# Four stages of a small vision network on one core: further matmuls without a reader in TensorE's pauses between the triangle product and the recurrence

## The reference

```python
# third block, on x normalized
a = sigmoid((x @ Wa1 + ba1) * (x @ Wa2 + ba2)); b = sigmoid((x @ Wb1 + bb1) * (x @ Wb2 + bb2))
g = sigmoid(x @ Wg + bg)
z = einsum('bikc,bkjc->bijc', a, b)
x = x + g * (_ln(z, ln2_g, ln2_b) @ Wz + bz)      # _ln over the 16 channels of z
# fourth block, on x normalized
def step(carry, xw_t):                            # 28 steps
    h, c = carry
    zi, zf, zo, zg = split(xw_t + h @ Wm)
    c_new = sigmoid(zf) * c + sigmoid(zi) * tanh(zg)
    h_new = sigmoid(zo) * tanh(c_new)
```

## Time and profile before

| what | value |
|---|---|
| median of three runs | 473.28 us (470.24 to 478.76) |
| the profiled execution | 475.85 us |
| its span, first to last instruction | 474.1 us |
| mean granted clock over the span | 0.901 |
| TensorE matmuls busy | 351.1 us (74%) |
| VectorE busy | 365.1 us (77%) |
| ScalarE busy | 299.8 us (63%) |
| GpSimd (POOL) busy | 233.9 us (49%) |

### The profile page before, as it was taken

One profiled execution on the slowest core, in us unless ns is written; L12 is line 12 of the kernel. 1 busy time (PEld: TensorE's weight loads), 2 busy tenths in 40 slices (PEclk: granted clock), 3 DMA queues, 4 the chain that ended last, 5 costly groups with the idle time before them and its releaser, 6 DMA issues. The chain is left out here.

```text
span 474.1 us, 10021 instructions
## 1 busy us (share of the span) xinstructions
PE 351.1 (74%) x3480; PEld 230.4 (49%) x3480; DVE 365.1 (77%) x679; ACT 299.8 (63%) x583; POOL 233.9 (49%) x217
## 2 busy tenths in 40 slices
PE   5149888896789785985877647666795829888885
PEld 4037676675665332142233213222483519877774
DVE  3799999999797388799787999997576685544443
ACT  4327788887785899578758946347985253333432
POOL 4526868775673324966972999567081130000000
PEclk9997999998899999599897885768999668999999
DMA  6110000000223231022000000000030000111111
GB/s 147 5 18 3 3 1 0 0 1 0 59 60 70 51 87 29 1 60 58 1 0 1 0 1 0 0 0 1 3 68 3 1 0 11 20 19 22 22 19 24
DMA packets 24044, 10.29 MB, mean 22 GB/s; under 512 B 20576, under 2 KB 22368, under 8 KB 24016
## 3 DMA queue, kind: packets, MB, share of 16 engines
q1 hardware_dynamic: 23888, 9.93, 10.3%
q0 software_dynamic: 128, 0.01, 0.2%
HBM read 2.00 MB, written 1.61 MB: 8 GB/s over the span
## 5 line engine op out<-in xcount | busy, mean ns | idle before, releaser
L480 POOL TENSOR_TENSOR Pr<-Pr,rc 128x392 f32<-128x392 f32 x64 | 54.4, 883 | 32.2 <-DVE rc L1826 32.2
L511 POOL TENSOR_TENSOR YA<-YA,hC 128x784 f32<-128x784 f32 x27 | 51.7, 1914 | 32.4 <-DVE hC L1910 31.5
L1349 PE MATMUL pair<-BCf,sel 96*128 96x392 bf16 x128 | 38.4, 394 | 35.0 <-DVE Hs L1894 30.8
L1894 DVE TENSOR_TENSOR_SCAN Hs<-dA,pair 128x784 f32<-128x784 f32 x32 | 57.1, 1785 | 1.0
L1193 PE MATMUL pair<-ident,Pr 128*128 128x128 f32 x256 | 41.1, 293 | 13.2 <-ACT PT L715 9.0
L1349 PEld LDWEIGHTS pair<-BCf,sel 96*128 96x128 bf16 x128 | 10.2, 105 | 74.0 <-issue 71.6
L1193 PEld LDWEIGHTS pair<-ident,Pr 128*128 128x128 f32 x256 | 29.2, 146 | 25.1 <-ACT PT L715 15.8
L1887 DVE TENSOR_TENSOR pair<-DU,pair 128x784 f32<-128x784 f32 x32 | 31.1, 973 | 10.6 <-PE pair L1349 10.3
L715 ACT ACTIVATE PT<-pair 128x392 f32<-128x392 f32 x64 | 31.4, 497 | 5.9 <-PE pair L1193 5.6
L724 ACT ACTIVATE Pr<-Ts 128x392 f32<-128x392 f32 x64 | 32.5, 536 | 3.4 <-DVE Ts L1810 3.4
L1804 DVE TENSOR_REDUCE mx<-pair 128x8 f32<-128x392 f32 x64 | 32.6, 550 | 1.6 <-PE pair L1150 1.4
(11 more groups left out here) (262 smaller groups left out, 928.8 us busy)
## 6 DMA issues: line engine op xcount, KB each, us to landing
SX<-XP SPq DMA_DIRECT2D x48, 112.2 KB
XT<-in_x SPq DMA_DIRECT2D x4, 392.0 KB, 5.0
out<-Os SPq DMA_DIRECT2D x28, 56.0 KB, 1.8
AD<-Aa SPq DMA_DIRECT2D x4, 196.0 KB
NB<-in_L_conv_x_proj_w SPq DMA_DIRECT2D x4, 3.0 KB
DW<-in_L_conv_dw SPq DMA_DIRECT2D x4, 1.1 KB
vec<-in_L_conv_b_qkv POOLq DMA_DIRECT2D x3, 0.5 KB, 5.8
W<-in_L_conv_w_qkv SPq DMA_DIRECT2D x1, 48.0 KB
```

What stands on the lines that cost most here:

```text
L480: eng.tensor_tensor(pg, pg, bcast(rc[:, g, :], 2, WT), ALU.mult).then_inc(pn_r, 1)
L511: eng.tensor_tensor(y, y, hC[:, n % NHC, :], ALU.add).then_inc(g_ya, 1)
L1349: ins = eng.matmul(SPREAD[s][:, columns(h)], sel[:, n, :], upper(BCf[:, c % 2, s, columns(h)]), start=True, stop=True)
L1894: eng.tensor_tensor_scan(Hs[:, n % 2, :], dA[:, n % NA, :], SPREAD[0], 0.0, ALU.mult, ALU.add).then_inc(v_s, 1)
```

## The change

TensorE's program alone is changed. After `variance(1)` (t_v at 2) it issues nine matmuls of `spare` instead of three, then waits for t_c at 3 and issues five more. Between `turn_z(0)` and `turn_z(1)` it waits for t_v at 3 and issues eight. After `final(1)` it issues four groups of eight into bank 5: behind t_y at 4, behind `biases`, behind l_mv at 2, and behind l_mv at 3. Then, as before, it waits for the normalized data.

```diff
             eng.wait_ge(t_v, 1)
             spare(3, 7)
             eng.wait_ge(t_v, 2)
-            spare(3, 7)
+            spare(9, 7)
+            eng.wait_ge(t_c, 3)
+            spare(5, 7)
...
             eng.wait_ge(t_gd, 8)
             eng.wait_ge(t_n, 2)
             turn_z(0)
+            eng.wait_ge(t_v, 3)
+            spare(8, 7)
             eng.wait_ge(t_n, 3)
             eng.wait_ge(t_nd, 1)
             turn_z(1)
...
             eng.wait_ge(t_y, 4)
+            spare(8, 5)
             eng.wait_ge(t_ye, 4)
             biases(0, 0)
             biases(1, 1)
+            spare(8, 5)
+            eng.wait_ge(l_mv, 2)
+            spare(8, 5)
+            eng.wait_ge(l_mv, 3)
+            spare(8, 5)
             eng.wait_ge(l_xn, J - 1)
             eng.wait_ge(l_x3, 1)
             inputs(0, 0)
```

## The result

The changed kernel takes 472.98 us in the median of 22 executions (467.71 to 475.02). The kernel before, run as often, takes 476.94 us (470.24 to 479.19). The ratio is 0.9939, with a 95% interval of 0.9909 to 0.9968: about 2.9 us less, between 1.5 and 4.3. Taken from the two medians it is 4.0 us; the ratio says less because it leaves out the executions that were over 1.5% above the fastest of their kernel, nine before and four after. The three runs shown ahead of the prediction had a median of 473.28, so they were low by 3.7 us.

A forecast was written before the change was run, and what follows sets the result against it. The chain of waits lies mainly on VectorE here, passing through half-clock TensorE in two places. Gains of 2.5 us (`turn_z(1)`, `final`) and 1.1 us (recurrence) make 3.6; 473.28 - 3.6 = 469.7 us, range 465.3 to 475.0.

The forecast's parts named there:

- The clock is the mechanism, in two places: A faster TensorE helps at `turn_z(1)` with `final`'s first half, 2.5 us, and at the recurrence's first step, 1.1 us.
- `turn_z(1)` gained: The second transposes, before `final`, take at most 1.05 us instead of 1.73; 0.75 us gained with the pipeline's end.
- The first half of `final`: The first 64 records of `final`, 4.63 us at half clock, gain 1.75 us (1.5 to 2.0) at full clock.
- First inputs to gates: At the recurrence's start, 2.94 us becomes 1.86 as in step 2: 1.1 us gained, upper end 1.5.
- The costs put at zero: Added matmuls before `turn_z(0)`, between the transposes and behind `final` fit TensorE's pauses; bank conflicts and code loading also 0.
- The idle time in front of `turn_z(1)`: After the eight added matmuls, 0.7 us of slack remains before VectorE's scaling of the last image releases `turn_z(1)`.
- The sum for the median: Whole kernel: 2.5 + 1.1 = 3.6 us off the three runs' median of 473.28 gives 469.7 us.
- Rival 1: In the 1.8 to 1.9 us pause before the recurrence the clock falls again; 1.1 us lost, 470.8; chance 0.23.
- Rival 2: The clock falls before `final` all the same; only the recurrence's 1.1 us remain, 472.2; chance 0.10.
- Rival 3: Added matmuls at half clock delay the transposes in TensorE's order: +4.9 us, 478.2; chance 0.05.
- Rival 4: The transposes stay slow, `turn_z(1)` at 1.73 us; 2.85 us gained, 470.4; chance 0.02.
- Code loading: TensorE's longer program may add a stop like the 0.82 us one at its loop's entry: 0 to 0.8, taken as 0.

The follow-up runs named there:

- e1_front: The changed kernel without the four groups of eight behind `final`; ratio to the kernel before 0.9989 (0.9951 to 1.0026).
- e3_no_last: The changed kernel without its last group of eight, behind l_mv at 3; ratio to the kernel before 0.9990 (0.9949 to 1.0030).
- e2_back: The changed kernel with the front undone, only the four groups behind `final` added; ratio to the kernel before 1.0053 (1.0012 to 1.0093).
- e5_nine_more: The changed kernel with 18 instead of nine matmuls in the group after t_v at 2; one execution, 115.3 us from triangle product to end.
- e10_conv_only: The kernel before with 14 matmuls without a reader ahead of `conv(2)` and 12 within it; median 471.21 us, ratio to the kernel before 0.9929.
- e7_no_mid: The changed kernel without the eight matmuls between `turn_z(0)` and `turn_z(1)`; one execution, 117.3 us from triangle product to end.
- e11_conv_pause: The changed kernel with 14 matmuls in its last group and 14 in the pause ahead of `conv(2)`, none within it; ratio to the kernel before 0.9876.
- e8_last14: The changed kernel with 14 instead of eight matmuls in its last group; median of six 473.13 us, ratio to the kernel before 0.9857.

## Why the prediction was right or wrong

**The clock is the mechanism, in two places: right.** The two places add up in the trace: 2.55 us up to the first inputs, 1.3 us in the first step, 3.9 in all, where 2.5 + 1.1 = 3.6 was forecast. e1_front has the first without the second, and e3_no_last against the changed kernel shows the second by itself. e2_back was to show it too and did not, since the clock fell there all the same.

**The terms.** `turn_z(1)` gained 1.73 - 0.96 = 0.77 (forecast 0.75). The first half of `final` gained 4.63 - 2.83 = 1.80 (1.75), and VectorE kept up, as forecast: its four gatings run on in 2.54 us. Their row in the changed kernel:

```profile
376.24 2.54 DVE L2124 SCALAR_TENSOR_TENSOR Y<-pair,vec,Gt 128x392 f32<-128x392 f32 x4 [0.35 <-PE pair L1587]
```

First inputs to gates gained 2.94 - 1.63 = 1.31, not 1.1: in step 2, from which I took the 1.86 us, L1642 waits for the state (written until 397.86, L1642 starts at 397.92), which costs some 0.2 us that the first step does not need. The costs put at zero were zero: the transposes start 11.15 and 14.64 us behind the product, before 11.15 and 14.63. The idle time in front of `turn_z(1)` was 0.66 us (0.7 forecast), and e5_nine_more shows that the slack is real and finite.

**The sum for the median: the step that failed.** It reads "the forecast for a median is 473.28 - 3.6 = 469.7". The change of 3.6 us (ratio 0.9924) lies inside the measured interval, near the 4.0 between the medians and the 2.9 of the ratio. The level under it does not hold: 473.28 was the median of three executions, and 22 gave 476.94. The profiled execution, 475.85, was the nearer one, and 475.85 - 3.6 = 472.2 would have been 0.8 us off. Set against the level now known, 469.7 says 7.2 us less: 1.8 times the 4.0 us between the medians and 2.5 times the 2.9 us of the ratio. I used the spread of those runs to widen the range, which then held 472.98, and not to doubt the centre; that the range held is owed to its width. What spreads the runs was in the trace: the clock in the second block, at 5 tenths in slices 17 and 25, which the prediction passed over as "high through most of the span". In its place the runs showed a level that hangs on an earlier pause: with the pause in front of `conv(2)` filled and nothing else changed, the median is 471.21 against 474.71 of the kernel before beside it, and the scatter falls from 7.6 to 2.1 us (e10_conv_only). Not all of the scatter is explained by it; `conv(2)` itself begins anywhere from 186.4 to 189.0 us.

**Rival 1 (the clock falls again before the recurrence): it happens in some executions.** The rows named in its favour and against it, 1.81 us held and 2.18 us fell, were read as if a length of pause decided. It doesn't alone: a pause of 1.82 us in the same place held in the two profiles of the changed kernel and was followed by a fall in those of three kernels that differ from it ahead of the pause. I gave it 0.23 as an alternative for the median; it is rather a share of executions, and the three profiles lost 1.0 to 1.3 us each. That both profiles of the changed kernel held may be luck. What this takes from the gain of the whole time is not shown: the means of all 22 executions, 476.32 and 472.44, differ by 3.9 us, as much as the two tails, and with their scatter they could not tell 3.9 from 3.

**Rival 2** did not occur in any of ten profiles with both front groups, and occurred in full without the middle one (e7_no_mid). **Rival 3** did not occur; its mechanism, delay in order, is what e5_nine_more measured at full clock: 0.86 us for nine. **Rival 4**, by the rule of the Trainium skill (TensorE: Matmul & The Clock Gate, Part 4: PE-mode transpose), fell: seven took 0.96 us at a granted 1.00, so the trace does not agree with the page. Whether transposes alone would keep or raise the clock, no run here separates. **Code loading** cost nothing that shows: the stop at the loop's entry is 0.84 us, before 0.82.

## What to carry to other kernels

Cut the trace at the first changed instruction and compare from there; here the start of the product alone carries 6 us of scatter that the change doesn't touch, and a forecast should be given as a difference with the level taken from as many runs as there are. Matmuls without a reader pay where a stretch bound by TensorE follows a pause (this chain, and the second block's third convolution), cost nothing while they end before the next releaser, and are worth nothing where VectorE bounds, however low the clock. Fill the pause up to its end: with 1.82 us left, the clock held in two profiles and fell in three; with 0.53 us left it held in five of five.

## What the runs showed of the hardware that was not expected

A convolution of column-tiled matmuls (L1287, 96 x 32 weights) ran at 0.50 for 13.5 us with TensorE busy for all of them and did not bring the clock back; with the pause in front of it filled it kept the 1.00 at which it began, with or without other matmuls between its parts (e11_conv_pause, 9.5 us). Beginning at 1.00 is not enough: in e5_nine_more and e8_last14, behind the unfilled pause, its first part still ran at full clock (0.87 us), and the 0.50 came 0.9 and 1.1 us behind its start. `final`, also of 32-column tiles (L1585), did see the clock come back, 3.7 us behind its start in the kernel before and 3.3 to 4.3 us in the other profiles that began it at 0.50.

The clock fell inside some pauses and behind others. In the kernel before it fell 0.9 us into the 2.27 us in front of `turn_z(0)` and 1.9 us into the 8.50 us in front of the recurrence. In e3_no_last it was 1.00 through 4.18 us of idle time and fell in the first inputs, in e5_nine_more 1.2 us after they had begun. So a 0.50 in a row of stretches can name the place of the cost and not that of the cause: the pause is to be looked for ahead of it.
